# Expert sums of a mixture-of-experts layer gathered in two tables in place of three

## The reference

```python
    logits = xt @ router_w.T
    probs = jax.nn.softmax(logits.astype(jnp.float32), axis=-1)
    top_w, top_i = jax.lax.top_k(probs, K)                       # K = 8, E = 64
    top_w = top_w / jnp.sum(top_w, axis=-1, keepdims=True)
    comb = comb.at[jnp.arange(T)[:, None], top_i].set(top_w)
    def step(acc, ws):
        wg_e, wu_e, wd_e, we = ws
        h = jax.nn.silu(xt @ wg_e.T) * (xt @ wu_e.T) @ wd_e.T    # D = 512, F = 128
        return (acc + we[:, None] * h, None)
    routed, _ = jax.lax.scan(step, jnp.zeros_like(xt), (Wg, Wu, Wd, comb.T))
    shared = jax.nn.sigmoid(xt @ Wse.T) * (jax.nn.silu(xt @ Wsg.T) * (xt @ Wsu.T) @ Wsd.T)
...
x = x + _layernorm(_L0_attn_ref(_layernorm(x, axis=-1), ...), axis=-1)
x = x + _layernorm(_L0_ffn_ref(_layernorm(x, axis=-1), ...), axis=-1)
```

## Time and profile before

| | us |
|---|---|
| median of 3 runs (lowest, highest) | 1150.92 (1149.81, 1154.15) |
| the profiled execution | 1146.0 |
| its span, first to last instruction | 1144.1 |
| PE busy | 1064.7 (93%) |
| DVE busy | 672.1 (59%) |
| POOL busy | 598.9 (52%) |
| ACT busy | 503.8 (44%) |
| first scatter, last scatter | 591.03, 1090.22 |
| first load of the sums | 1094.13 |

### The profile page before, as it was taken

How to read it: one execution, slowest core, us unless ns; L and a number is a source line. 1 busy time by engine, 2 the same in 40 slices (tenths; PEclk the granted TensorE clock), 3 DMA queues, 4 the chain that set the end, 5 groups by cost and what they waited for, 6 DMA issues and landing times.

```text
span 1144.1 us, 24242 instructions
## 1 busy us (share of the span) xinstructions
PE 1064.7 (93%) x6269; PEld 722.2 (63%) x6270; DVE 672.1 (59%) x2308; ACT 503.8 (44%) x1419; POOL 598.9 (52%) x631
## 2 busy tenths in 40 slices
PE   5999899989999989989989999999999999999954
PEld 3556556655566645556667777777777777777721
DVE  5566566655666658869935555454454554544538
ACT  2666567656666763446632222222222222222224
POOL 4533343333343313321247787888888888788810
PEclk9899999999999999989999999999999999999978
DMA  9920000000000015110279999999999999998888
GB/s 324 337 107 1 3 1 1 1 3 1 1 1 1 2 51 217 56 46 2 74 239 230 238 225 266 260 248 276 274 267 264 257 264 292 272 252 175 159 283 321
DMA packets 68375, 180.05 MB, mean 157 GB/s; under 512 B 13456, under 2 KB 15248, under 8 KB 68176
## 3 DMA queue, kind: packets, MB, share of 16 engines
q0 software_dynamic: 38496, 93.08, 34.2%
q1 hardware_dynamic: 29808, 86.07, 21.4%
HBM read 119.85 MB, written 66.85 MB: 163 GB/s over the span
## 4 chain that ended last, share of the span: by engine, by line
PE 65%; DMA 15%; DVE 10%; issue 5%; POOL 3%; ACT 1%; DVEq 0%; POOLq 0%; SPq 0%; ACTq 0%
PE ps L760 15%; PE ps L1036 13%; DMA sum_rows<-x_t,idx 9%; PE ps L1047 7%; PE ps L819 7%; PE ps L877 5%; DMA x_t<-x_rows,idx 4%; PE ps L789 4%; PE ps L839 4%; PE ps L1029 4%; PE ps L774 2%; DVE low L1322 1%; POOL sum_rows L487 1%; DVE qkv_all L1326 1%; DVE low L1325 1%
## 5 line engine op out<-in xcount | busy, mean ns | idle before, releaser
L1036 PE MATMUL ps<-big,work 128*128 x1264 | 299.1, 380 | 0.0
L487 POOL DMA_INDIRECT sum_rows<-x_t,idx x157 | 250.2, 1593 | 58.5 <-issue 41.4
L1036 PEld LDWEIGHTS ps<-big,work 128*128 128x128 f32 x1264 | 228.0, 190 | 24.5
L760 PE MATMUL ps<-big 128*128 128x384 f32 x512 | 182.6, 501 | 1.0 <-ACT big L549 0.6
L482 POOL DMA_INDIRECT x_t<-x_rows,idx x152 | 150.0, 987 | 51.8 <-issue 24.1
L414 POOL TENSOR_TENSOR work<-qkv_all,rope_sb 128x256 f32<-128x256 f32 x64 | 46.6, 727 | 244.2 <-ACT qkv_all L554 244.2
L702 ACT ACTIVATE work<-ps 128x512 f32<-128x512 f32 x159 | 94.9, 597 | 170.7 <-PE ps L1029 169.1
L1047 PE MATMUL ps<-big,work 128*128 x314 | 160.5, 592 | 1.0 <-ACT attn_t L680 1.0
L1029 PEld LDWEIGHTS ps<-ident_sb,x_t 128*128 128x128 f32 x636 | 77.8, 141 | 95.1 <-issue 76.3
L1153 DVE CUSTOM_DVE_ANT_0 ps<-ps,mask_sb 128x128 f32<-128x128 f32 (+3 forms) x256 | 120.5, 512 | 23.5 <-PE ps L789 22.8
L573 ACT ACTIVATE work<-ps,neg_max 128x128 f32<-128x128 f32 (+3 forms) x256 | 132.3, 526 | 3.4 <-DVE neg_max L1153 2.4
(11 more groups left out here) (187 smaller groups left out, 1411.4 us busy)
## 6 DMA issues: line engine op xcount, KB each, us to landing
big<-experts SPq DMA_DIRECT2D x65, 768.0 KB, 7.1
sum_rows<-x_t POOLq DMA_DIRECT2D x6, 2048.0 KB, 16.2
big<-sum_rows SPq DMA_DIRECT2D x8, 768.0 KB, 9.9
x_rows<-work SPq DMA_DIRECT2D x16, 256.0 KB, 2.0
out<-x_sb SPq DMA_DIRECT2D x16, 256.0 KB, 5.6
x_sb<-x SPq DMA_DIRECT2D x3, 1024.0 KB, 10.5
x_t<-sum_rows SPq DMA_DIRECT2D x4, 768.0 KB, 13.3
attn_t<-sum_rows SPq DMA_DIRECT2D x4, 768.0 KB, 13.5
```

What stands on the lines that cost most here:

```text
L487: pool.indirect_dma_start(all_sums, bass.IndirectOffsetOnAxis(ap=idx[:, q, 1:2], axis=0), y_sb[q], None, bounds_check=last_sum, oob_is_err ...
L760: mm = pe.matmul(bank[:, 0:QKV], x_t[:, c, bass.ts(t, P)], wqkv_sb[:, c, g % G, :], start=(c == 0), stop=(c == DC - 1))
L1036: mm = pe.matmul(ps[:, 2 + p, 0:GATEUP], rows_t[:, p, c, :], w_ring[:, slot, c * GATEUP:(c + 1) * GATEUP], start=(c == 0), stop=(c == DC - 1))
```

## The change

The sums are gathered in two tables. Scatters alternate between them, so a scatter waits for the landing of the one two tiles back. The counts in the waits follow: a pass of six tiles brings each table three scatters (TURNS) where it brought two. The first tile that goes to table 0 is now tile 1 and was tile 2, and the wait for the stored shared results moves with it. Two zero fills are gone, each load at the end holds two rows per token in place of three, TensorE adds two and DVE makes one addition in place of two.

```diff
-TABLES = 3
+TABLES = 2
+TURNS = DEEP // TABLES
...
                 pool.wait_ge(s_y, t)
-                pool.wait_ge(s_scatter[table_of(c)], (j * 2 + (c // TABLES + 2)) * 16)
+                pool.wait_ge(s_scatter[table_of(c)], (j * TURNS + (c // TABLES + 2)) * 16)
                 pool.sem_inc(s_issue, 1)
                 scatter(c)
...
             pool.wait_ge(s_y, full * DEEP + (DEEP + 1))
-            pool.wait_ge(s_scatter[table_of(0)], (full * 2 + 4) * 16)
+            pool.wait_ge(s_scatter[table_of(0)], (full * TURNS + TURNS + 2) * 16)
...
             for p in range(TABLES):
-                pool.wait_ge(s_scatter[p], (full * 2 + (5 if p == table_of(0) else 4)) * 16)
+                pool.wait_ge(s_scatter[p], (full * TURNS + TURNS + (3 if p == table_of(0) else 2)) * 16)
...
                 dve.wait_ge(s_dn, t + 2)
                 dve.wait_ge(s_scatter[table_of(q)], r)
-                if q == 2:
+                if q == 1:
                     dve.wait_ge(s_ysh, 48)
...
-                    take_y(t - 1, c, (j * 2 + (c // TABLES + 1)) * 16)
+                    take_y(t - 1, c, (j * TURNS + (c // TABLES + 1)) * 16)
...
-            take_y(quads * DEEP, 0, (quads * 2 + 1) * 16)
+            take_y(quads * DEEP, 0, (quads * TURNS + 1) * 16)
...
                 step(dve.tensor_tensor(out=y, in0=y, in1=sums_of(i)[:, 1, :], op=ALU.add))
-                step(dve.tensor_tensor(out=y, in0=y, in1=sums_of(i)[:, 2, :], op=ALU.add))
```

## The result

| | before | after |
|---|---|---|
| median of 4 runs (lowest to highest), us | 1150.37 (1144.01 to 1154.15) | 1216.70 (1215.51 to 1221.96) |
| profiled execution, its span | 1146.0, 1144.1 | 1215.93, 1214.1 |

The change makes the kernel slower: ratio 1.0591, 95% interval 1.0534 to 1.0649. The forecast was 1225 us with 1178 to 1268.

What follows compares the result with a forecast made beforehand. TensorE and POOL were taken as within 2% of each other, with scatter landings about to bind. 63 + 10 + 0 + 5 + 3 - 7 = +74 us on 1146, 1225 us against the runs' median; range 1190 to 1255, wider 1178 to 1268.

Steps and rivals of the forecast that it cites:

- the drain: Last six scatters, with no gathers between them: two tables make their five steps 16 us in all, +5 us.
- the end: Loads and sums after the last scatter: smaller loads, fewer matmuls and fewer DVE additions, together -7 us.
- The zero fills: Filling the tables with zeros early on: four fills of 2 MB in place of six, gain nothing.
- p = 3.69 us with a landing of 6.6: Routed loop beside weight loads: period per tile when scatters wait two tiles back, against 3.21 us; cost 63 us.
- I add 0.07 us per tile: Routed loop: allowance for uneven landings, since short ones can't give back what long ones took; 10 us.
- Rival B: Routed loop: held scatters get larger relief, landing 5.9 us, period 3.35 us, +29 us, 1180 us in all; chance 0.10.
- about 0.8 us each: Sign expected in the profile: POOL's idle time before a scatter in the loop, put down to a scatter's landing.
- The traffic line: Routed loop: landing time follows DMA traffic, from 5.1 us at 159 GB/s to 7.3 us at 260 GB/s.
- Cost nothing beside POOL's: DVE's wait in take_y, for the landing four tiles back in place of six: no cost of its own.
- The start: First scatters: tile 1 in place of tile 2 waits for the stored shared results; +3 us, bounds 0 and 4.
- tile 2's follows a period of 3.2 later: First scatters: after tile 1's delayed scatter at 599.5 us, tile 2's comes 3.2 us later, within the +3 us.
- rival D: Routed loop: TensorE's granted clock falls as it idles; +34 us if a tenth of tiles ran lower, 1259 us; chance 0.02.

Runs made afterwards that it cites:

- experiment 1: Kernel before, three tables kept, but each scatter also waits for the landing of the scatter two tiles back: 1236.09 us, ratio 1.0796.
- experiment 4: Changed kernel with two tables, the 56 expert weight loads of the routed stage left out: 1143.55 us, ratio 0.9985 to the kernel before.
- Experiment 6: Changed kernel with two tables, each of the 56 routed-stage weight loads bringing only half its columns: 1178.88 us, ratio 1.0273 to the kernel before.
- experiment 9: Kernel before, three tables, scatters waiting for the landing two back: 1235.98 us; with take_y also waiting for the landing four back: 1220.71 us.
- experiment 3: Changed kernel with two tables, but take_y waits for the landing six tiles back in place of four: 1233.52 us, ratio 1.0752 to the kernel before.
- experiment 5: The changed kernel itself, measured again on another chip: 1212.47 us, ratio 1.0584 to the kernel before.
- experiment 7: Changed kernel with two tables, the last store of shared results issued in front of the 768 KB weight load: 1209.50 us, ratio 1.0569 to the kernel before.

## Why the prediction was right, and where it wasn't

The mechanism and its place held. L514's wait sets the pace (experiments 1 and 4). The 0.8 us from landing to start, read off two rows, is 0.74 to 0.88 in 46 of 52 cases. The loop without loads cost nothing, the drain 3.8 us for 5, and the end gave 7. TensorE's clock in the loop stayed at 0.99. The zero fills gave nothing that the profiles show: the first scatter starts 1.8 us earlier, but in the other profiles it starts at 588.6 to 591.4 us with three tables and at 587.1 to 590.8 with two.

**The period of the loop was hit by luck.** It was forecast as 3.69 + 0.07 = 3.76 us, and the mean of scatters 6 to 133 is 3.76. But both terms are off. The step "p = 3.69 us with a landing of 6.6" took the landing too long: its mean was 6.16 us (median 6.0), so the half of landing plus 0.82 is 3.49 us. The step "I add 0.07 us per tile" took the unevenness too small. It had a quarter of the landings below 5.6 us, by half a us; it was 53 of the 128, by 0.6 in the mean. 3.76 - 3.49 is 0.27 us per tile, of which the six starts that came later still make 0.04. With the landing right and the 0.07 kept, the same sum would have said about 1198 us. Experiment 6 shows the second miss again: (5.68 + 0.82) / 2 = 3.25 us against a measured 3.50. That the loop's cost is 68.3 and not 73 is counting: the forecast took 132 periods over 3.21 us, and scatters 4 to 134 are 130 periods of 3.75 over 3.22.

The reason for the unevenness lies in which scatters land fast. Of those 128, the 75 that followed 3.2 us after the one before landed after 6.56 us in the mean, the 23 that were held to a gap below 4.2 us after 6.03, and the 30 held longer after 5.25. A scatter that was held long lands below the 5.6 us that it may use, and what it has to spare is lost, because POOL's own work takes 3.18 us per tile. Landings below 5.6 us leave 0.15 of the 0.27 us unused in this way. Another 0.11 is left by longer landings: a held scatter moves the next one too, since POOL works in order, and where the next one is late already, the landing that it waits for could have been longer at no cost. Rival B's reason (a held scatter finds the gather before it further on) agrees with the direction, but the runs don't separate it from a weight load that has meanwhile ended. B as a forecast (1180 us) was wrong, though the landing came out between its 5.9 us and the forecast's 6.6: the relief is largest where it isn't used.

One sign was read wrong in advance. POOL was not idle "about 0.8 us each" before its scatters: 76 of the 128 were not held at all, and the 52 late ones found it idle for 1.7 us in the mean.

**The traffic line** between 159 and 260 GB/s gives 6.5 us at 224 GB/s; the mean was 6.16. At 193 GB/s it gives 5.8, and the mean was 5.68. It was a fair guess, no law: it was drawn through two points with landings of three scatters in flight. The landing's forecast range of 6.2 to 7.0 missed the median of 6.0.

**"Cost nothing beside POOL's"**, of the wait in `take_y`, was right that it doesn't hold the scatters, and wrong in its sign: it saves 15 us (experiment 9; experiments 1 and 3 agree). DVE and TensorE wait there as forecast (DVE 147 us, in 90 of 134 tiles).

**The start** was +6.4 us for +3. Of these, 4.9 lie between scatters 0 and 1 (9.45 us for 4.59), where the forecast had 3.9: scatter 0 came 1.8 us earlier, but the store's landing let `take_y` go only 0.8 us earlier. Another 1.8 lie between scatters 2 and 3 (4.98 us for 3.18). There, "tile 2's follows a period of 3.2 later" left out that TensorE stands still behind DVE and goes on at a lower clock. The profiles tell what that costs: in the 7 us after scatter 1 the granted clock was 0.61 here, 0.80 in the same kernel's second profile (experiment 5) and 1.00 in experiment 7, where the idle time was shorter; scatter 3 followed scatter 2 after 4.98, 3.65 and 3.18 us. It is rival D's mechanism at another place, and its size differs between two profiles of one kernel.

The Trainium skill's rule for a DMA (*DMA: Bandwidth & Descriptors*, "Anatomy of one DMA — SWDGE (gpsimd) path") gives a scatter 4.2 us with POOL's part, an estimate, and hence nothing held. The lone last scatter landed after 3.67 us in the kernel before and 3.06 after the change, which is near that. The 5.1 us beside gathers and the 6.0 to 7.3 beside weight loads are above it, and they decide here.

## What to carry to other kernels

Where several transfers take buffers or tables in turn, compare landing under load + release to start with the period: the quotient, rounded up, is how many are needed. The landing must be taken from the stretch with the most other traffic: here 7.3 + 0.8 against 3.19 needs three, and 5.1 + 0.8 needs two. When a wait binds, don't use the mean landing over the count: the landings that are short can't pay back the long ones, and a held transfer delays the next one too; that was 0.27 us of 0.55 here. Ask also what a wait holds back beside its own engine, before loosening it.

## What the runs showed that I had not expected

A wait that was added made the kernel faster by 15 us. What goes with it is when the weight loads start. SP issues one when TensorE is through with an expert. In the changed kernel 42 of the 56 loads start 1.6 to 2.4 us after the start of a scatter (worked out from each load's and each scatter's start). With the looser wait in `take_y` (experiment 3) the counts by steps of 0.8 us from a scatter's start are 16, 9, 6, 3, then 11 from 3.2 to 4.0 and 11 beyond. With three tables and both waits it is 44 of 56. Where the loads are in step with POOL, the scatters held longer than a gap of 4.2 us land after 5.0 to 5.3 us in the mean; where they are spread, after 5.6 to 6.1. Of the 0.12 us per tile between experiment 3 and the changed kernel, 0.07 is the longer mean landing (6.30 us for 6.16), and the rest is more room left unused. That the step is the cause was not tried apart: no run moved the loads alone.
